# Loading the expert tiles' rows with a transposing DMA instead of turning them on TensorE

## The reference

```python
x = x + gnn(layernorm(x), adj)                 # 4096 x 128
z = layernorm(x)
gate = z @ Wg.T + bg; top 2 of 8 experts, softmax over the two
for e in range(8):
    h = relu(z @ W1[e].T + b1[e])              # 128 -> 512
    y = h @ W2[e].T + b2[e]                    # 512 -> 128
    out += combine[..., e:e+1] * y
x = x + out
```

## Time and profile before

| | |
|---|---|
| median of 3 runs | 497.34 us (496.49 to 498.46) |
| the profiled execution | 501.04 us, of which the span 498.9 us |
| PE busy | 416.5 us, 83% of the span |
| DVE busy | 377.9 us, 76% |
| ACT busy | 338.8 us, 68% |
| POOL busy | 244.5 us, 49% |
| first tile's load to the last store's landing | 332.58 to 478.81 us |
| mean granted TensorE clock | 0.946 |

### The profile page before, as it was taken

One profiled execution on the slowest core, in us unless ns is written; L12 is line 12 of the kernel. 1 busy time (PEld: TensorE's weight loads), 2 busy tenths in 40 slices (PEclk: granted clock), 3 DMA queues, 4 the chain that ended last, 5 costly groups with the idle time before them and its releaser, 6 DMA issues. The chain is left out here.

```text
span 498.9 us, 8921 instructions
## 1 busy us (share of the span) xinstructions
PE 416.5 (83%) x2671; PEld 258.2 (52%) x2672; DVE 377.9 (76%) x928; ACT 338.8 (68%) x345; POOL 244.5 (49%) x355
## 2 busy tenths in 40 slices
PE   1999969999899699999975899669889898989900
PEld 0555424444344245544433454337788897979900
DVE  5999977989999999679667999955885554645426
ACT  2799993799979879799946689703555555645400
POOL 2059940001601883754743587125477776564620
PEclk9999979999999999999987999797999999998975
DMA  8749766786755768668555577214233332222149
GB/s 241 277 171 341 300 264 227 254 294 263 252 197 226 253 211 269 250 215 310 201 191 184 201 237 267 93 40 103 71 109 120 103 108 79 62 87 61 33 179 326
DMA packets 31149, 95.63 MB, mean 192 GB/s; under 512 B 5548, under 2 KB 18148, under 8 KB 22912
## 3 DMA queue, kind: packets, MB, share of 16 engines
q1 hardware_dynamic: 19920, 80.06, 46.5%
q0 software_dynamic: 6048, 12.72, 7.7%
q10 hardware_dynamic: 5136, 2.30, 1.6%
HBM read 83.28 MB, written 12.67 MB: 192 GB/s over the span
## 5 line engine op out<-in xcount | busy, mean ns | idle before, releaser
L1366 PE MATMUL bank<-tbuf,g_sb 128*128 128x512 f32 x512 | 238.6, 614 | 1.0 <-ACT g_sb L1125 0.7
L1366 PEld LDWEIGHTS bank<-tbuf,g_sb 128*128 128x128 f32 x512 | 96.7, 197 | 111.5 <-issue 104.0
L865 DVE SCALAR_TENSOR_TENSOR marks<-abuf,marks 128x2048 bf16<-128x2048 int32 x56 | 130.6, 2332 | 1.6 <-DVE marks L865 0.5
L1105 ACT ACTIVATE tbuf<-abuf 128x2048 f32<-128x2048 f32 x64 | 121.4, 1897 | 10.5 <-DVE key L991 7.9
L1109 ACT ACTIVATE tbuf<-tbuf 128x2048 f32<-128x2048 f32 x64 | 122.3, 1910 | 2.0
L615 POOL DMA_INDIRECT routed_rows<-aug,slots x64 | 80.6, 1259 | 56.2 <-DVE base L843 37.1
L644 POOL DMA_INDIRECT expert_rows<-abuf x78 | 76.7, 983 | 47.7 <-issue 26.4
L1068 DVE SCALAR_TENSOR_TENSOR tbuf<-bank,tbuf 128x512 f16<-128x512 f32 x78 | 51.3, 687 | 31.2 <-ACT tbuf L1224 31.2
L1224 ACT ACTIVATE tbuf<-bank 128x512 f16<-128x512 f32 x78 | 46.2, 596 | 30.8 <-PE bank L1483 29.6
L1502 PE MATMUL bank<-w2h,tbuf 128*128 x312 | 54.7, 220 | 3.5 <-DVE tbuf L1068 3.5
L1503 PE MATMUL bank<-w2l,tbuf 128*128 x312 | 54.6, 220 | 0.0
(11 more groups left out here) (235 smaller groups left out, 527.1 us busy)
## 6 DMA issues: line engine op xcount, KB each, us to landing
abuf<-in_adj_tiles SPq DMA_DIRECT2D x64, 1024.0 KB, 5.3
abuf<-routed_rows SPq DMA_DIRECT2D x41, 130.0 KB
wstage<-in_w POOLq DMA_DIRECT2D x16, 256.0 KB, 6.4
tbuf<-expert_rows SPq DMA_DIRECT2D x8, 512.0 KB, 7.2
out<-xres ACTq DMA_DIRECT2D x8, 256.0 KB, 6.2
expert_rows<-abuf POOLq DMA_INDIRECT x78, 2.4
routed_rows<-pad SPq DMA_DIRECT2D x9, 130.0 KB
routed_rows<-aug,slots POOLq DMA_INDIRECT x64, 4.2
```

What stands on the lines that cost most here:

```text
L865: dve.scalar_tensor_tensor(mark, bits_in, 1.0, mark, ALU.min, ALU.add).then_inc(s_raw, 1)
L1105: act.activation(tbuf[:, n % NBUF, :, :], abuf[:, n % NBUF, :, :], ACT.Square).then_inc(s_sq, 1)
L1366: last = pe.matmul(ps_feat[ib % 2][:, :], g_sb[:, c, :], tbuf[:, buf, cc, :], start=(c == 0), stop=(c == C - 1))
```

## The change

**The load.** Two DMAs fill a tile's buffers. The first is a transposing DMA: it reads the 128 words of 256 rows as 256 x 256 halves and puts them into SBUF turned, as `xhl[:, u]`, 128 partitions by (high or low part) by 256 rows. The second reads the two last words of each row, 8 bytes, as `xmeta`. Both add to the same semaphore, so PE waits for twice the count. There are eight buffers of both. `turn_x`, `copy_x`, their semaphores and the PSUM bank are gone, and `layer1` reads the loaded tile. In the DMA of `xmeta`, row s·128 + p of a tile belongs to partition p.

**The loops.** All 39 tiles are written out on SP, POOL, DVE, ACT and PE. PE loads experts' numbers before tiles 0, 8, 16, 17, 24 and 32. The unused tiles 39 and 40 are gone.

**The bias.** One product of 256 columns, reading the bias row twice, stands for two of 128.

```diff
+        xhl = a_flat[:, 0:NX * TS].bitcast(fp16).rearrange("p (n v s) -> p n v s", n=NX, v=2)
+        xmeta = a_flat[:, 2048:2048 + NX * 4].rearrange("p (n s w) -> p n s w", n=NX, s=2)
-                sp.dma_start(xld[:, u, :, :], xs[bass.ds(row, TS), :].rearrange("(p s) w -> p s w", p=P)
+                sp.dma_start(xhl[:, u, :, :], xs[bass.ds(row, TS), 0:D].bitcast(fp16), transpose=True
+                             ).then_inc(s_xl[u], 16)
+                sp.dma_start(xmeta[:, u, :, :], xs[bass.ds(row, TS), D:ROW].rearrange("(s p) w -> p s w", p=P)
                              ).then_inc(s_xl[u], 16)
-            for t in range(F0):
+            for t in range(NT):
                 cut_h(t, t % 2)
-                copy_x(t + 2, t % 2)
                 route_steps(FFN + t)
-            with dve.Fori(0, (NT - F0) // 2) as g:
...
             def layer1(t, q, e, fresh=False):
-                pe.wait_ge(s_xc, t + 1)
+                u = t % NX
+                pe.wait_ge(s_xl[u], (t // NX + 1) * 32)
...
-                for s in range(2):
-                    pe.matmul(ps_y[:, s * D:(s + 1) * D], ones_h[:, :],
-                              b2_hl[:, bass.ds(e, 1), :].rearrange("p o d -> p (o d)"),
-                              start=(s == 0), stop=False, skip_group_check=True)
+                pe.matmul(ps_y.rearrange("p (s d) -> p s d", s=2), ones_h[:, :],
+                          b2_hl[:, bass.ds(e, 1), :].to_broadcast([P, 2, D]), start=True, stop=False,
+                          skip_group_check=True)
...
-                pe.wait_ge(s_xl[(t + 2) % NX], ((t + 2) // NX + 1) * 16)
-                turn_x(t + 2, (t + 2) % NX)
...
+                if t + 1 < NT and (t + 1 == N1 or (t + 1) % NX == 0):
+                    table_e, end = (first_e, N1) if t + 1 < N1 else (tile_ei, NT)
+                    experts = experts[-1:] + load_experts(nc, pe, table_e, t + 1, min(NX - (t + 1) % NX, end - t - 1))
+                    k0 = t
+                if t + 1 < NT:
+                    layer1(t + 1, (t + 1) % 2, experts[t + 1 - k0], fresh=t < 1)
                 layer2(t, t % 2, experts[t - k0], fresh=t < 1)
-            with pe.Fori(0, NG) as g:
```

More of the change, by code:

```diff
@@ L478, in _ @@
             sp.sem_inc(s_spare, 1)
[L479 to L489, removed]
+            for t in range(N1, NT):
                 sp.wait_ge(s_sc[t % NX], t // NX * 32)
@@ L636, in _, with store_tile @@
                     scatter(i, rerouted)
-            def store_tile(t, u, loop=True):
+            def store_tile(t, u):
                 pool.wait_ge(s_yo, t + 1)
-                if loop:
-                    pool.sem_inc(s_spare, 1)
                 for s in range(2):
                     pool.indirect_dma_start(
-                        ys, bass.IndirectOffsetOnAxis(ap=xld[:, u, s, D:D + 1].bitcast(i32), axis=0),
+                        ys, bass.IndirectOffsetOnAxis(ap=xmeta[:, u, s, 0:1].bitcast(i32), axis=0),
                         ysb[:, u, s, :], None, bounds_check=2 * N - 1, oob_is_err=False).then_inc(s_sc[u], 16)
-            for t in range(F0):
-                store_tile(t, t % NX, loop=False)
+            for t in range(NT):
+                store_tile(t, t % NX)
                 if t == LAST_SCATTER:
                     scatter(NB - 1, routed)
-            with pool.Fori(0, NG) as g:
-                for j in range(NX):
-                    store_tile(g * NX + F0 + j, (F0 + j) % NX)
         @block.vector
@@ L1056, in _ @@
                 chain[:] = before_if
[L1058 to L1062, removed]
             def cut_h(t, q):
@@ L1070, in cut_h @@
                                              ALU.max, ALU.subtract).then_inc(s_hs, 1)
-            copy_x(0, 0, fresh=True)
-            copy_x(1, 1, fresh=True)
-            for t in range(F0):
+            for t in range(NT):
                 cut_h(t, t % 2)
-                copy_x(t + 2, t % 2)
                 route_steps(FFN + t)
@@ L1230, in y_out @@
                     last = act.activation(ysb[:, u, s, :], ps_y[:, s * D:(s + 1) * D], ACT.Copy,
-                                          scale=xld[:, u, s, D + 1:D + 2])
+                                          scale=xmeta[:, u, s, 1:2])
                 last.then_inc(s_yo, 1)
-            for t in range(F0):
+            for t in range(NT):
                 relu_h(t, t % 2, fresh=t < 2)
@@ L1238, in _ @@
                 route_steps(FFN + t)
[L1239 to L1243, removed]
             y_out(NT - 1, (NT - 1) % NX)
@@ L1505, in layer2 @@
                 last.then_inc(s_y, 1)
-            for t in range(2):
-                pe.wait_ge(s_xl[t], 16)
-                turn_x(t, t, fresh=t == 0)
             experts = load_experts(nc, pe, first_e, 0, NX)
+            k0 = 0
             layer1(0, 0, experts[0], fresh=True)
-            for t in range(F0):
+            for t in range(NT):
                 route_steps(FFN + t)
-                pe.wait_ge(s_xl[(t + 2) % NX], ((t + 2) // NX + 1) * 16)
-                turn_x(t + 2, (t + 2) % NX)
                 if t + 1 == N1:
```

50 lines of the change are left out of this document (7 added, 43 removed).

## The result

| | before | changed |
|---|---|---|
| median | 496.91 us (496.24 to 498.46, 4 runs) | 488.98 us (485.38 to 491.11, 4 runs) |
| ratio, 95% interval | | 0.9846 [0.9801, 0.989] |
| the profiled execution | 501.04 us, span 498.9 | 491.11 us, span 489.4 |
| first tile's load issued | 332.58 | 332.69 |
| last store issued | 476.69 | 467.24 |

The kernel is faster by 7.9 us; I had forecast 13.7. The two profiled executions differ by 9.5 us in their spans, all of it between the first load and the last store: 476.69 - 332.58 = 144.1 us before, 467.24 - 332.69 = 134.6 us after.

A forecast was written before the change was run, and what follows sets the result against it. PE was taken as the bound from the gate near 389 us on, at 2.99 us a tile. The terms 5.2 + 5.5 + 0.9 + 0.8 + 1.3 = 13.7 us took the median 497.34 to 483.6 us; range 479 to 525.

The forecast's parts named there:

- step 4: PE's wait for tile 14's load, freed by tile 6's store: iteration 13 begins at 383.8 instead of 389.0, 5.2 us ahead.
- step 6: PE's idles before tiles 17, 23 and 31: shorter when written out, 0.9 us; avoiding the lower clock, 0.8 us.
- Bias: PE's bias products, one of 256 columns for two of 128: zero, under 1 us in either direction.
- Start: Layer1 of tile 0 no longer waits for transposes and copies: starts at 336.8 instead of 338.46, 1.6 us earlier.
- DVE's copies: Eight copies leave the chain during the last routing: 2.6 us; tile 6's store from 374.6, 3.6 us earlier.
- 25 iterations: Iterations 14 to 38, where PE is the bound: 0.22 us saved in each, 5.5 us.
- The unused layer1: Layer1 of tile 39, in front of the last layer2, goes: 1.3 us.
- The load's pace: Condition: a tile's two DMAs keep up with 2.77 us; SP has room unless the transposing DMA's issue takes over 1.5 us.
- A: Rival: transposing loads cannot keep pace, PE waits for them at layer1; 541 us at 4.6 us a load; chance 0.23.
- B: Rival: loads' pace between 3.0 and 3.5 us, saved transposes return as PE's waits; 494 to 498 us; chance 0.09.
- C: GpSimd's stores become the bound if the last scatter comes no earlier; only caps the gain, at 483; forecast with C 0.68.

The follow-up runs named there:

- e1: Changed kernel with the eight empty-row DMAs moved from SP's queue to ACT's, one per iteration 8 to 15; 542.54 us, ratio 1.0 to the kernel before, chip 12.
- e11: Changed kernel with two transposing DMAs of 128 rows per tile instead of one of 256; 546.86 us, ratio 1.011 to the kernel before, chip 14.
- e12: The kernel before, run again with no edit for a profile, on chip 4; 496.13 us, and 500.43 beside it.
- e5: The changed kernel run again with no edit on chip 12; 537.41 us, ratio 0.9955 to the kernel before.
- e9: Changed kernel with two PSUM tiles used in turn for layer2's result; 528.13 us, ratio 0.9751 to the kernel before, chip 14.

## Why the prediction was right or wrong

The direction was right: the kernel is faster, and PE's stream lost its transposes at the forecast price. The size was not, 7.9 us for 13.7, and 9.5 in the profiled pair. And the number came nearer than the working deserved: the gate (step 4) lost 6.7 us against the forecast, and the loop (step 6), a half guess, gave 3.2 more than I took. Of the 9.4 us below, the new load gives 5.5 - 1.5 = 4.0, and what is written out, with the unused layer1 gone, 3.2 + 1.7 + 1.3 = 6.2, less 0.8 for a wait elsewhere. So the larger part is not the transposes'; that is a reading of two traces, and neither part was run alone on such a chip. By its own steps:

1. **Bias**: nothing is seen against zero; the stream's 2.76 us a tile is the forecast 2.77.

2. **Start**: layer1 of tile 0 at 337.12, forecast 336.8. But tile 1 was late too (1.05 us at 341.76), behind an issue of 2.87 us, and all its products ran at the lower clock; before, the clock rose during that tile. The first bias product came at 344.30, and before at 343.76: the forecast gain of 1.6 was gone within one tile and had become a loss of 0.5.

3. **DVE's copies** are gone and gave what was forecast. The last block's places were assigned at 364.83, and not at 366.77: 1.9 us earlier instead of 3.6. The store of tile 6 went out at 376.88 instead of 374.6. Tile 9's bias product was 2.6 us ahead (374.21, before 376.81) instead of 4.2. Counted from the 0.5 us behind of step 2, these are gains of 2.5 and 3.1 us, for 2.0 and 2.6 forecast: what is missing is the start's.

4. **The gate** is the step that failed. I let tile 14's load hang on the store of tile 6 and on SP's few tenths behind it, and forecast iteration 13, which needs that tile, at 383.8. SP had not come that far. The load that held PE up was tile 13's; it waited for no store, but stood behind 13 loads at 3.03 us and 8.6 us of empty rows. Had it gone out at the old 378.64, it would have landed 3.41 us later at 382.05, 0.7 us after PE asked for it at 381.34; the other 3.05 us came with SP's longer issues. I had not summed the queue. PE waited 3.89 us, and the 5.30 us from 385.23 to 390.53 were 2.54 more than a tile at the full clock. 3.89 + 2.54 = 6.4 of the 6.7 us by which iteration 13 came later than forecast (390.53). Instead of 5.2 us ahead, it was 1.5 behind the kernel before (389.01). That this wait was SP's issue and not the landing is shown by the rows: the chain runs on SP up to 381.69, and the landing took 3.41 us. That a shorter queue would give it back was not shown, since e1 moved the wait and ran where the kernel before takes 540 us. Nor would all 6.4 us come back. By the rows the old gate stands close behind: the second store of tile 6 at 378.18, landed in about 2.4, then 0.80 and 3.41 as above, puts tile 14 at an estimated 384.8, and PE would ask for it at 381.34 + 2.76 = 384.1.

5. **25 iterations**: 0.22 to 0.23 us each, 5.5 us, as forecast; PE busy 7.00 of 7.00 us.

6. **The loop** gave more than forecast: PE's idles are 1.19, none, and 0.55 us, 1.74 for 4.90, so 3.2 where I took 0.9. The read without a branch kept its price before tile 17 (1.19, before 1.05), the two former loop heads fell from 1.76 and 2.09 to none and 0.55, below the 1.05 that I had left for each. The stretch at the lower clock near 448 us is gone, 1.7 where I took 0.8.

7. **The unused layer1**: 1.3, as forecast.

Beside these, PE waited 0.8 us once for `y_out`. The sum is -1.5 + 5.5 + 3.2 + 1.7 + 1.3 - 0.8 = 9.4 us, measured 478.81 - 469.37 = 9.4 at the last landing.

8. **The load's pace** was the wrong test. I wrote that SP has room unless the transposing DMA takes over 1.5 us to issue. At the median it takes 1.21, and a load takes SP 384.35 - 381.69 = 2.66 us, just under PE's 2.77. But over the first 13 loads the longer issues bring it to 3.03 a tile, so there the condition itself failed by a little. And even where it holds it says only that SP does not fall behind further: SP builds up hardly any lead in the 13 loads, and then 8.6 us of other issues stand in its queue. A pace is not enough: the queue's own sum, from its start to the item, must be made. The DMA engines stayed hidden, as forecast. The changed kernel's q1, 340:450:

```profile
q1 hardware_dynamic: 30626, 5.86, 30.7%
```

0.307 x 16 x 110 / 30626 = 17.6 ns a piece, below both rows that I had (26 and 59), and hidden.

Here the two rules of the Trainium skill can be weighed. The Trainium skill, "Advanced Engine Details and Errata", section "X-Bar Transpose (TRN2)", holds a transposing DMA as fast as a regular one. From issue to landing the trace is near that: 385.10 - 381.69 = 3.41 us against 3.07, with the second DMA's issue in it; no run here measures the rate of a long transfer. The Trainium skill, "VectorE: DVE Perf Modes", section "The three transpose paths", has 1309 ns for a block by DMA. Here a tile of four blocks was issued in 1213 ns and half a tile in 1185, and loads followed each other every 2.6 us, so the 5.2 us a tile that I worked out from it did not come.

**The rivals.** A named the place (PE's wait for the load, by SP's issue) and asked for it tile after tile beyond 3.5 us; after the first two tiles it came once. e11, at 3.9 us of issue a tile, shows it many times and ends slower than the kernel before. B did not come. C did not decide: the last store was issued at 467.24, past what GpSimd alone would need (376.88 + 32 x 2.60 + 1.30 = 461.4).

## What to carry to other kernels

A DMA that does work for the engines can cost its issuer several times what the plain one costs (here 1.21 us for 0.33), once an instruction. So give it as many bytes as it takes, and look how much of the issuer's time was waiting before, for that is all the room there is. Sum the issuing queue from its start up to each item that somebody waits for, other issues between them included. An experiment that moves an item out of a queue must be followed to whoever awaits that item, or the wait only changes its place. And a saving on the bounding engine counts only where that engine is the bound: before a change is judged, look whether its stream runs without gaps on the chip at hand. Last, when a total comes out near the forecast, add up the steps: here two large misses had opposite signs.

## What the runs showed of the hardware

- The transposing DMA's issue on SP: 1.21 us for 256 rows of 512 bytes (the changed kernel), 1.19 us for 128 rows (e11), 0.33 us for the plain load that it replaced (the kernel before); medians.
- After 3.89 us without a product, PE ran at the lower of its clock levels for 5.3 us (products of 256 columns 0.21 us apart, and 0.11 after it).
- The same program takes about 497 us in the first comparison (496 and 500 beside e12) and 540 on two other chips (12 and 14). The first 330 us are alike; then ACT is released 1.92 us after PE's last product instead of 0.26 (e5, the changed kernel). The eight issues of empty rows take SP 15.4 to 18.5 us on chip 12 instead of 8.58, but 9.5 and 8.9 in e9 and e11 on chip 14. With two PSUM tiles for the result the changed kernel takes 528 us there and with one 537, on two chips.
